# The sums ahead of a digit move from DVE to POOL, in six of the seven searches of a top-k attention kernel

## What is computed

```python
scores = jnp.einsum('bhqd,bhkd->bhqk', q, k) * scale
sparsity = scores.max(axis=-1) - scores.mean(axis=-1)
_, top_idx = jax.lax.top_k(sparsity, U)              # U = 307 of 4096
q_sel = jnp.take_along_axis(q, top_idx[..., None], axis=2)
attn = jax.nn.softmax(jnp.einsum('bhud,bhkd->bhuk', q_sel, k) * scale, axis=-1)
out = jnp.zeros_like(q).at[bi, hi, top_idx].set(jnp.einsum('bhuk,bhkd->bhud', attn, v))
x = _layernorm(x + out.transpose(0, 2, 1, 3).reshape(b, l, D) @ Wo + bo)
x = _layernorm(x + sigmoid(xr @ W_r.T) * (square(relu(xk @ W_k.T)) @ W_v.T))   # xr, xk mix each token with the one before
```

## Time and profile before

| | us |
|---|---|
| median of 3 runs | 3449.08 |
| lowest and highest | 3445.66, 3450.98 |
| the profiled execution, its own time | 3456.68 |
| its span, first to last instruction | 3454.9 |
| first and last L1154 in it | 776.5, 3164.8 |

### The profile page before, as it was taken

How to read it: one execution, slowest core, us unless ns; L and a number is a source line. 1 busy time by engine, 2 the same in 40 slices (tenths; PEclk the granted TensorE clock), 3 DMA queues, 4 the chain that set the end, 5 groups by cost and what they waited for, 6 DMA issues and landing times.

```text
span 3454.9 us, 58997 instructions
## 1 busy us (share of the span) xinstructions
PE 3099.2 (90%) x15985; PEld 1433.1 (41%) x15985; DVE 2950.1 (85%) x5969; ACT 2873.2 (83%) x6445; POOL 1482.1 (43%) x2619
## 2 busy tenths in 40 slices
PE   6999999998899998998999888899988898897678
PEld 3334333343344433433444344444444443344466
DVE  4989988899979888888899888888988898886578
ACT  5889888889779999899899877699977699894555
POOL 2210022100136643553456356665555653447744
PEclk8999999999999999999999999999999999997899
DMA  6333222216021251141021251211142131013122
GB/s 178 80 100 113 64 75 82 82 30 18 15 44 32 39 33 31 33 33 32 19 36 31 46 48 42 49 37 35 31 41 48 35 33 32 14 20 15 19 79 69
DMA packets 262608, 163.63 MB, mean 47 GB/s; under 512 B 167877, under 2 KB 241797, under 8 KB 258181
## 3 DMA queue, kind: packets, MB, share of 16 engines
q1 hardware_dynamic: 254181, 156.41, 25.0%
q0 software_dynamic: 6144, 1.37, 0.5%
q10 hardware_dynamic: 1952, 2.10, 0.2%
HBM read 111.86 MB, written 47.86 MB: 46 GB/s over the span
## 4 chain that ended last, share of the span: by engine, by line
ACT 29%; PE 27%; issue 20%; DVE 19%; POOL 2%; DMA 1%; ACTq 0%; DVEq 0%; SPq 0%; POOLq 0%
ACT AB L941 21%; DVE JK L1100 11%; PE CP L669 8%; PE DP L673 7%; ACT E L979 5%; ACT msk L962 2%; PE PV L780 1%; PE PV L781 1%; PE BP L765 1%; PE BP L615 1%; DVE VF L1311 1%; DVE fst L1270 1%; DVE SPr L1100 1%; PE PV L803 1%; PE PV L615 1%
## 5 line engine op out<-in xcount | busy, mean ns | idle before, releaser
L1100 DVE CUSTOM_DVE_ANT_0 JK<-DP,AB 128x1024 bf16<-128x1024 f32 x2048 | 2468.0, 1222 | 366.5 <-DVE SPr L1100 129.9
L941 ACT ACTIVATE AB<-CP 128x512 f32<-128x512 f32 x4096 | 2226.6, 598 | 282.7 <-PE CP L669 234.2
L669 PE MATMUL CP<-KS,QS 128*128 128x512 f16 x4096 | 1424.0, 388 | 94.7 <-ACT AB L941 20.1
L673 PE MATMUL DP<-KS,QS 128*128 128x512 f16 x4096 | 1236.9, 384 | 61.1 <-DVE SPr L1100 54.6
L1506 POOL TENSOR_TENSOR SCR<-E 128x307 f16<-128x307 f32 x953 | 661.8, 707 | 585.1 <-ACT E L979 578.3
L669 PEld LDWEIGHTS CP<-KS,QS 128*128 128x128 f16 x4096 | 392.3, 96 | 887.5 <-ACT AB L941 752.7
L673 PEld LDWEIGHTS DP<-KS,QS 128*128 128x128 f16 x4096 | 360.9, 98 | 386.0 <-DVE SPr L1100 171.0
L979 ACT ACTIVATE E<-BP 128x307 f32<-128x307 f32 x871 | 379.6, 436 | 30.3 <-PE BP L765 29.2
L1355 POOL TENSOR_SCALAR SCR<-SCR 128x48 f16<-128x48 f16 (+2 forms) x122 | 49.2, 403 | 540.6 <-DVE SCR L1066 316.4
L765 PE MATMUL BP<-QT,KA 128*128 128x307 f16 x871 | 258.3, 297 | 20.4 <-ACT QT L971 18.4
L780 PE MATMUL PV<-E,XT 128*128 128x307 bf16 x512 | 161.0, 315 | 26.6 <-POOL SCR L1506 25.9
(11 more groups left out here) (369 smaller groups left out, 2997.3 us busy)
## 6 DMA issues: line engine op xcount, KB each, us to landing
KS<-KTC SPq DMA_DIRECT2D x256, 128.0 KB
QS<-QSC SPq DMA_DIRECT2D x512, 64.0 KB
KA<-KTC SPq DMA_DIRECT2D x128, 128.0 KB
QN<-SCR SPq DMA_DIRECT2D x16, 544.0 KB, 3.5
SCR<-in_L_attn_x SPq DMA_DIRECT2D x16, 512.0 KB, 6.3
AO<-E SPq DMA_DIRECT2D x16, 512.0 KB, 7.1
VF<-in_L_attn_x SPq DMA_DIRECT2D x64, 128.0 KB, 2.2
VF<-AO SPq DMA_DIRECT2D x64, 128.0 KB, 2.2
```

The costliest lines, as they stand in the source:

```text
L669: pe.matmul(o, qs, ks[j][:, 1, :], start=True, stop=True).then_inc(sc_c, 1)
L673: r = pe.matmul(o[:, 512 * j:512 * j + 512], qs, ks[j][:, 0, :], start=True, stop=True)
L941: act.activation(AB[p % 3][:, 512 * j:512 * j + 512], BANK["C%d" % j], ACT.Abs).then_inc(ab_full, 1)
L1100: dve.tensor_tensor_reduce(out=JK[p % 2][:], in0=BANK["D%d" % u], in1=AB[p % 3][:], scale=1.0, scalar=-3.0e38, op0=ALU.add, op1=ALU.max, a ...
```

## The change

A new semaphore `sel_nx` is added. POOL gets a stage `digit` of its own: in the searches with `on == "A"`, at the place of the `digit` step in the list, it waits until the digit before has left its limits (`sel_lim`), adds `steps` and the lower limit into `ahead_of`, and raises `sel_nx`. DVE no longer issues that sum there; it waits for `sel_nx` ahead of L1161. The last search keeps the sum on DVE.

```diff
--- before.py
+++ after.py
@@ -499,6 +499,7 @@
         sel_thr = sem("sel_thr")
         sel_st, sel_cmp, sel_pe, sel_lim, sel_key, sel_m = (sem(n) for n in (
             "sel_st", "sel_cmp", "sel_pe", "sel_lim", "sel_key", "sel_m"))
+        sel_nx = sem("sel_nx")
         sel_sl, sel_f, sel_ob, sel_tk, sel_oa, sel_ix = (sem(n) for n in (
             "sel_sl", "sel_f", "sel_ob", "sel_tk", "sel_oa", "sel_ix"))
         arr, ah_pe, ah_act, s_pe, ex_act, el_g, el_d = (sem(n) for n in (
@@ -1150,7 +1151,7 @@
                 plain = i + 1 < len(DIGITS) and i + 1 != LOW
                 if i and i != LOW:
                     dve.wait_ge(sel_lim, 16 * g + i)
-                if plain:
+                if plain and on == "D":
                     dve.tensor_scalar(ahead_of[0:rows, :], steps[0:rows, i + 1, :], now[0:rows, 0:1], None, ALU.add)
                 dve.wait_ge(sel_pe, SEL0[g] + 2 + i)
                 q = seq.mark(dve.tensor_scalar(met[0:rows, 0:w], BANK[bank][0:rows, 0:w], goal, None, how, ALU.add,
@@ -1158,6 +1159,8 @@
                 dve.wait_ge(q_dve, q)
                 count = met[0:rows, 3:4]
                 if plain:
+                    if on == "A":
+                        dve.wait_ge(sel_nx, 14 * g + (i + 1 if i < LOW else i))
                     dve.scalar_tensor_tensor(out=new[0:rows, :], in0=count.broadcast_to([rows, 4]), scalar=step,
                                              in1=ahead_of[0:rows, :], op0=ALU.mult, op1=ALU.add).then_inc(sel_lim, 1)
                     return
@@ -1434,6 +1437,15 @@
                 pool.wait_ge(s_hi, k + 1)
                 pool.tensor_tensor(lo, s, hi, ALU.subtract).then_inc(s_lo, 1)
 
+            def digit(g, i, on, bank):
+                if on == "A" and i + 1 < len(DIGITS) and i + 1 != LOW:
+                    rows = 16 * GROUPS[g][2]
+                    if (g, i) == (0, 0):
+                        pool.wait_ge(consts, 3)
+                    after(pool, sel_lim, 16 * g + i)
+                    pool.tensor_scalar(ahead_of[0:rows, :], steps[0:rows, i + 1, :], limits_of(i)[0:rows, 0:1], None,
+                                       ALU.add).then_inc(sel_nx, 1)
+
             def slots(g):
                 n = GROUPS[g][2]
                 si, bi = (q[:].rearrange("p t h -> p (t h)")[:, 0:NT * n] for q in (sloti, slb))
@@ -1603,7 +1615,7 @@
                     pool.wait_ge(f_r2, k + 1)
                     pool.tensor_scalar(fo[k % 4], fo[k % 4], r[:, 0:1], r[:, 1:2], ALU.mult, ALU.add).then_inc(f_o3, 1)
 
-            stages = dict(vset=vset, vones=vones, qzero=qzero, split=split, slots=slots, ob=ob, qgzero=qgzero, gath=gath, arr=arrange,
+            stages = dict(vset=vset, vones=vones, qzero=qzero, split=split, digit=digit, slots=slots, ob=ob, qgzero=qgzero, gath=gath, arr=arrange,
                           st=st, put=put, f1=f1, f2s=f2s, f3=f3, f5=f5, f6k=f6k, f7=f7, f8=f8, f9=f9)
             setup()
             for stage, *args in plan:
```

## The result

The changed kernel takes **3489.68 us** (median of 4 runs, 3485.24 to 3492.39) against 3447.76 us of the kernel before in the same batch: a ratio of **1.0119, interval [1.0107, 1.0131]**, or +41.9 us. A second measurement, made later beside two experiments, gives 3496.31 against 3445.49: 1.0144 [1.0126, 1.0162], +50.8 us. The forecast was slower, by 14.9 us: the sign came true, and the size is off by a factor of about three (2.8 and 3.4); both times lie above the range of 3453 to 3474.

The account below looks back on a forecast made before the run. ACT was taken to bound the attention stretches and a chain of waits the feed-forward ones. Late sums cost 9.9 + 8.3 us, less 3.3 gained: +14.9 on the median of 3449.1, so 3464 us, range 3453 to 3474.

Parts of the forecast that it names:

- The bound of each kind of stretch: Beside attention ACT paces the rounds, busy 105.7 of 108 us; beside feed-forward nobody is full, a chain of waits.
- 18 places foreseen: Of 84 sums, POOL is still busy at 18: six beside attention (9.9 us), twelve beside feed-forward (8.3 us).
- those beside attention with 0.14 us of margin: Three sums where POOL ends only 0.14 us ahead: late by 0.2, inside the 0.4 that is hidden.
- The places beside attention: Six late sums in groups 1, 2 and 5, behind POOL's transfers or subtractions: 0.48 to 2.27 each, together 9.9 us lost.
- the gain beside feed-forward: Four digits where PE and ACT wait for L1161 gain 0.7 us each, three more 0.14: together 3.3 us.
- The term of the sum's price: POOL's sum takes 0.22 us; DVE's L1161 can start 0.34 us after POOL's previous operation (0.24 to 0.38).
- Whether L1161 inherits the hold is open: At the four gaining digits L1161 takes 0.16 or 0.71 us; the longer removes the gain, sum 3 us higher.
- Two more are late by 0.5 with nobody waiting close behind: Two of the twelve late sums beside feed-forward; half is counted, 0.5 us in all.
- 0.49 us each: Five late sums beside feed-forward behind POOL's variance chain, delaying L1323, for which PE already waited 1.58 us: 2.45 us.
- The feed-forward part swallows its delays: Rival: PE and ACT make up the feed-forward delays, 6.6 us left, 3456 us, no difference; chance 17%.
- DVE's time is the bound: Rival: rounds are paced by DVE, so 14.2 us come off, 3435 us, faster; chance 6%.
- POOL's chain is late too: Rival: 28 feed-forward sums also delay what DVE and PE take from POOL, 6.7 us more, 3471 us; chance 16%.

Follow-up runs that it names:

- experiment 4: Changed kernel, but POOL makes each sum at the digit's first compare step, some rounds before it is needed: 3449.33 us, ratio 0.9996 to the kernel before.
- before's second trace: The kernel before, unchanged, measured and traced once more: 3447.11 us, span 3445.4 instead of 3454.9.
- the places filled: Changed kernel plus 14 unread matmuls on PE ahead of 18 bank claims in groups 3 and 4, 16 hitting the meant waits: ratio 1.0079, +29.0 us.
- both cuts made: Changed kernel with a plain digit's count in PSUM and unread PE matmuls ahead of 18 claims in groups 3 and 4: ratio 1.0069, +23.9 us.
- experiment 3: Kernel before, DVE keeping its own sums, plus 84 POOL sums into a tile nobody reads and no DVE wait for them: 3456.94 us, ratio 1.0022.

## Why the prediction was wrong in size

*Right.* The bound of each kind of stretch. DVE's time gives nothing that the launch shows (experiment 4). Where POOL is late: 18 places foreseen, 21 found; the other three, waits of 0.48 to 0.58 us, are those beside attention with 0.14 us of margin. The places beside attention to a tenth: 1.98 us of ACT's wait at group 1's digit 0 for a forecast of 1.99, +1.27 at its later one for 1.25. No loss in group 0, which is 0.7 us shorter (rounds 512 to 592; before's second trace 0.1 longer). Nothing for SP. And the gain beside feed-forward: the four waits of PE fell from 2.88 to 2.16 us, 0.72 each for a forecast of 0.7. With hold and clock out of the way, windows 3 and 4 together grow by 6.0 us for a forecast of 5.

*The term of the sum's price* ("So DVE's L1161 can start 0.34 us after POOL's previous operation ends (0.24 to 0.38)") is low. POOL's 80x4 sum takes 0.30, not 0.22, and L1164 starts 0.45 behind the transfer. That is 0.1 us in each of 21 places, 2 us. The Trainium skill ("GPSIMD Engine Reference", section 3.1), which I set aside, has POOL at about twice DVE; the trace shows 0.30 against 0.22, a factor of 1.4, between the rule and my row.

*The step "Whether L1161 inherits the hold is open"* was asked of the wrong digits. At the four of the gains L1164 takes 0.16 us, the lower answer. But I bounded a hold by 0.71, one POOL operation, and looked for it only there. It fell on four other digits: on the "Two more are late by 0.5 with nobody waiting close behind", of which I took half, 0.5 in all, and on two whose sum is in time, counted with 0.14 of gain at most. There L1164 takes 2.41 and 2.06, 1.65 and 1.69 us, for the whole run of POOL. The price: 5 us by the medians (29.0 against 23.9 with and without it, with intervals that overlap), 5.9 us in the traces over the rounds of these four digits (1.6, 1.4, 1.5 and 1.4). The trace of before had a warning in its last search, which I didn't read, where POOL runs on as well:

```profile
3160.06 1.45 DVE L1161 SCALAR_TENSOR_TENSOR test<-met,ahead_of 48x4 f32<-48x4 f32 x1
```

The rule that I leaned on, of the Trainium skill ("SBUF — State Buffer", "Who interferes with whom"), has whoever issues first keep the ports for the whole instruction. The trace agrees in the earlier trace rows, where L1161 ends with the operation that it met, and has more at the four digits: at digit 10 L1164 is not let in when the operation that it met ends at 2108.06, but at 2110.03, with the sixth.

*The largest failure is in no term at all.* I priced a delay of 0.49 us ahead of L1323 at "0.49 us each", that is, a microsecond of waiting at a microsecond. Of the 18 filled or missed places of groups 3 and 4, PE waited 1.6 to 1.8 us at eight before, 2.88 at four and under 1 us at six; now it waits 1.8 to 2.7 at all of them, and at many the next two rounds run at half clock, +1.2 to 1.5 us a place. From 3 slow places it went to 10 and 16. Priced by the runs: 41.9 and 50.8 us of the change, less 29.0 with the places filled, make **13 to 22 us**, a difference between batches that carries the intervals of both (some 6 to 7 us either way). The trace of before gave a hint that I did not use: the waits of 1.58 us lie in a stretch of clock 1.00, but behind two of its four waits of 2.88 us the clock is 0.50 (group 4, digits 1 and 10), so the range should have been open to more such places.

Group 2's window, 8.1 for 5, has the same thing beside attention. After its digit 0 PE waited 3.08 us and ran at 0.50; before has clock 1.00 through the whole window. No run has fillers there, so its share of the 3 us is not separated:

```profile
1542.12 1.03 PE L674 MATMUL DP<-KS,QS 128*128 128x512 f16 x2 [3.08 <-DVE SPr L1101]
```

```profile
1542.00:1544.00 2.00, 1.88 (x6) 0.89 (x7) 1.88 (x5) 1.33 (x4) 0.00 (x0) 0.50 1.86 4
```

*The sum as the runs price it:* late sums about 24 us (both cuts made: 23.9, of which the windows show 20), hold 5, half clock 13 to 22, the rest up to the 41.9 and 50.8 measured. Of the 24 the forecast had 14.9. The windows have 5 of the other 9: 3 in group 2, 2 in the rest, as much as the price of the sum explains. Some 4 us lie outside the windows and I can't place them all; about 1 us stands in the last search, whose sums stay on DVE: it is 0.8 us longer in after and 0.03 in before's second trace.

*The rivals.* "The feed-forward part swallows its delays" is refuted: that half alone costs 27.2 us. "DVE's time is the bound" is refuted by the sign. "POOL's chain is late too", nearest in its time, was right in sign for another reason. The fastest way out, the sums early, only returns to the time of before: no version here beats it.

## What to carry to other kernels

Before moving a small operation to an idle engine, ask where in that engine's order it lands, not how busy the engine is: 84 sums of 0.3 us on an engine at 43% cost 42 to 51 us in one place of its order and nothing a few rounds earlier. Price a delay at the engine that it makes wait, including what that engine does when it comes back: where TensorE already waited 1.58 us here, half a microsecond more cost 1.8. And look at what the helping engine does next to the operation that takes its result: two of the four long holds began just as the result was handed over, while POOL went on to its next work.

## What the runs showed of the hardware

- A small DVE operation whose inputs are both in SBUF can be held through a whole run of POOL operations that follow each other without a gap: 2.41 us behind six of them, 1.86 behind five in experiment 3. With one input moved to PSUM it takes 0.16 us in the same place. It isn't always so: in before it was let in after one operation (0.71 us) or at once (0.20 at 2114.68) with POOL going on. What decides stays open.
- After idling 2.0 to 2.5 us PE came back at the lower clock in 4 of 8 watched places in one trace and 8 of 8 in another of the same kernel, for 2 to 4 us. With fillers ahead of the wait, in none of 16, in two traces. It isn't only the length of the wait: in before a wait of 2.88 us was followed by full clock and another of 2.88 us in group 4 by half, and three of four unfilled waits of 2.69 to 2.76 us were followed by full clock when the places around them were filled. What decides between them stays open.
- The same kernel can gather a different number of such places from run to run (10 and 16), which moves its median between batches by more than its interval.
